# A decoder layer on one core: the first half's experts started inside the last cross-attention batch, with GpSimd splitting the first weights

## What is computed

```python
x = x + self_attention(layernorm(x))           # 16 heads of 64, causal
x = x + cross_attention(layernorm(x), ctx)     # 16 heads of 8, softmax over 256 keys
x = x + ffn(layernorm(x))

# ffn: 8 experts, the best two of each token
scores = xn @ Wr + br;  indicator = one_hot(top_k(scores, 2)).sum(-2)
weights = softmax(where(indicator > 0, scores, -inf))
for i in range(8):
    h   = relu((xn * indicator[..., i:i+1]) @ W1[i] + b1[i])     # 128 -> 512
    out = out + (h @ W2[i] + b2[i]) * weights[..., i:i+1]        # 512 -> 128
```

## Time and profile before

| | us |
|---|---|
| median of 3 runs | 348.15 |
| lowest, highest | 346.92, 350.82 |
| the profiled execution, its time | 347.81 |
| the span of its records | 346.0 |
| outside the span | 1.81 |

### The profile page before, as it was taken

How to read it: one execution, slowest core, us unless ns; L and a number is a source line. 1 busy time by engine, 2 the same in 40 slices (tenths; PEclk the granted TensorE clock), 3 DMA queues, 4 the chain that set the end, 5 groups by cost and what they waited for, 6 DMA issues and landing times.

```text
span 346.0 us, 5393 instructions
## 1 busy us (share of the span) xinstructions
PE 301.5 (87%) x1852; PEld 212.2 (61%) x1869; DVE 214.7 (62%) x452; ACT 190.4 (55%) x525; POOL 91.2 (26%) x130
## 2 busy tenths in 40 slices
PE   6799999999988997988688367776999999799995
PEld 2677777767865784556234123334778678578884
DVE  4768563746488848745877267446766876556661
ACT  2679767478466634664365258684553454336350
POOL 7990550320112009302400490313421300000000
PEclk9999999999999998999899699999999999899999
DMA  8800035501000100010029920000000000100001
GB/s 244 175 2 2 2 52 67 66 3 45 0 2 13 35 1 3 3 46 2 3 64 366 282 72 4 2 0 2 0 1 2 0 1 0 32 0 0 3 0 30
DMA packets 14911, 14.06 MB, mean 41 GB/s; under 512 B 2643, under 2 KB 10915, under 8 KB 14883
## 3 DMA queue, kind: packets, MB, share of 16 engines
q1 hardware_dynamic: 13300, 12.92, 15.1%
q10 hardware_dynamic: 1584, 0.80, 0.8%
HBM read 9.94 MB, written 0.52 MB: 30 GB/s over the span
## 4 chain that ended last, share of the span: by engine, by line
PE 65%; DVE 16%; DMA 4%; ACT 4%; issue 3%; SPq 3%; POOL 2%; another core or an unknown queue 0%; DVEq 0%; ACTq 0%; POOLq 0%
PE ps L592 6%; PE ps L594 6%; PE ps L593 6%; PE ps L666 6%; PE ps L699 4%; PE ps L711 4%; PE ps L868 4%; PE ps L869 4%; PE ps L870 4%; DMA w_raw<-in_L_ffn_b 3%; PE ps L744 3%; DVE mneg L1233 3%; PE ps L780 3%; PE ps L673 2%; PE ps L701 2%
## 5 line engine op out<-in xcount | busy, mean ns | idle before, releaser
L987 ACT ACTIVATE p<-ps,negmax 128x256 f32<-128x256 f32 (+1 forms) x128 | 52.6, 425 | 26.5 <-DVE negmax L1202 26.2
L1314 DVE SCALAR_TENSOR_TENSOR hid_lo<-ps,hid_hi 128x512 fp32r<-128x512 f32 x64 | 41.8, 685 | 23.3 <-ACT hid_hi L1051 23.3
L1233 DVE TENSOR_REDUCE mneg<-ps 128x2 f32<-128x512 f32 x64 | 42.3, 683 | 21.6 <-PE ps L744 20.9
L1016 ACT ACTIVATE px<-ps 128x512 f32<-128x512 f32 x64 | 35.1, 598 | 23.9 <-PE ps L765 22.1
L1202 DVE TENSOR_REDUCE negmax<-ps 128x2 f32<-128x512 f32 (+1 forms) x48 | 33.0, 687 | 20.6 <-PE ps L668 13.2
L1051 ACT ACTIVATE hid_hi<-ps 128x512 fp32r<-128x512 f32 x64 | 35.0, 596 | 8.1 <-PE ps L594 7.6
L744 PE MATMUL ps<-k_st,q_mem 128*128 128x256 bf16 x128 | 25.5, 283 | 12.3 <-DVE mneg L1233 11.5
L1046 ACT CAST x_hi<-x_f 128x512 fp32r<-128x512 f32 x16 | 9.9, 620 | 38.8 <-DVE x_f L1304 38.8
L973 ACT CAST t_hi<-ps 128x512 fp32r<-128x512 f32 x32 | 18.7, 591 | 19.5 <-PE ps L594 18.5
L592 PE MATMUL ps<-x_hi,w_hi 128*128 128x512 f32 x64 | 26.4, 412 | 2.2 <-DVE hid_lo L1314 1.4
L987 ACT ACTIVATION_READ_ACCUMULATOR p<-ps,negmax 128x1 f32 x128 | 26.6, 208 | 0.0
(11 more groups left out here) (191 smaller groups left out, 665.1 us busy)
## 6 DMA issues: line engine op xcount, KB each, us to landing
w_raw<-in_L_ffn_W SPq DMA_DIRECT2D x1, 2048.0 KB, 8.6
w_last<-in_L_ffn_W SPq DMA_DIRECT2D x1, 2048.0 KB, 14.5
k_st<-k_part SPq DMA_DIRECT2D x12, 128.0 KB
q_mem<-q_part SPq DMA_DIRECT2D x48, 32.0 KB
w_in<-in_L_attn_W_qkv ACTq DMA_DIRECT2D x2, 384.0 KB, 6.3
...
```

The source lines that it names most:

```text
L987: last = act.activation(dst, bank[:, n * i:n * i + n], ACT.Exp, bias=negmax[:, kt, h:h + 1], accum_out=psums[:, kt, h:h + 1])
L1016: act.activation(px[:, (g // 2) % 2, c0:c0 + 512], ps[:, k % 3, :], ACT.Exp, scale=SCALE_X).then_inc(s_px, 1)
L1233: dve.tensor_reduce(mneg[:, qt, :].rearrange("p (r g) -> p r g", r=2)[:, :, g], ps[:, max_bank[("MX", b, u)], :].rearrange("p (h k) -> p h ...
L1314: dve.scalar_tensor_tensor(hid[1][:, k % 2, c, :], ps[:, H_BANK[c], :], 0.0, hid[0][:, k % 2, c, :].bitcast(F32), ALU.max, ALU.subtract).t ...
```

## The change

1. **Memory.** `hid` keeps one run instead of two, both parts in the place of `q_mem0`, so that `q_mem1` (batches 2 and 3) stays whole while experts run. `w1_last` becomes a ring of three experts.
2. **Order.** `WS` moves from the eight slots of batch 2 to slots (1, 4), (1, 6), (2, 6) and expert runs 0 to 4. In batch 2 the output units of batch 1 and in batch 3 those of batch 2 come a slot earlier, `NT(0)` moves to (2, 7), `RT(0)` to (3, 0), `GT(0)` to (3, 2), `WT(0)` to (3, 3), `X(0)` to (3, 4). Slots 6 and 7 of batch 3, their `CO`, and `oT0`, `oT1`, `wo` of batch 2 and all output units of batch 3 stand between the chunks of runs 0 to 2. `W2` and the units of the second half shift likewise.
3. **Second product by chunks.** `Y(k-1, c)` stands ahead of `H(k, c)`, for each c. `relu_high` waits for the one chunk it overwrites.
4. **Banks.** Batch 3's scores use two banks instead of three, runs 0 and 1 have two hidden banks instead of four, and the last two output products share bank 3.
5. **GpSimd.** The low part of W1 is made on GpSimd (`first_low`) instead of DVE; `first_weights`, `first_low`, `second_weights` and `norm_3` alternate in a written order. PE waits for the low part of its own expert only.
6. **SP's queue.** Three last rows instead of all at once, then b2, a wait for W1, b1, the maxima of batch 2, W2, two last rows, the maxima of batch 3, the other three.

```diff
+LAST_RING = 3
...
-        w_in, q_mem0, hid_hi = overlay([("w_in", 4096, F32)], [("q_mem0", 8192, BF16)], [("hid_hi", 4096, F32R)])
+        w_in, q_mem0, hid_hi, hid_lo = overlay([("w_in", 4096, F32)], [("q_mem0", 8192, BF16)],
+                                               [("hid_hi", 2048, F32R), ("hid_lo", 2048, F32R)])
...
-        wk_mem, g_hi, ctxT, k_f, q_mem1, hid_lo = overlay(
+        wk_mem, g_hi, ctxT, k_f, q_mem1 = overlay(
             [("wk_blk", 2048, F32), ("g_hi", 2048, F32R)], [("ctxT", 1024, F32), ("k_f", 1024, F32)],
-            [("q_mem1", 8192, BF16)], [("hid_lo", 4096, F32R)])
-        hid = [w[:, :].rearrange("p (r c n) -> p r c n", r=2, c=NC) for w in (hid_hi, hid_lo)]
+            [("q_mem1", 8192, BF16)])
+        hid = [w[:, :].rearrange("p (c n) -> p c n", c=NC) for w in (hid_hi, hid_lo)]
...
-        px, w1_last, _, w2_hi, g_lo, t_hi, t_lo = overlay(
-            [("px", 4096, F32), ("w1_last", 4096, F32)], [("px_too", 4096, F32), ("w2_hi", 4096, F32R)],
+        px, w2_hi, g_lo, t_hi, t_lo = overlay(
+            [("px", 4096, F32), ("w2_hi", 4096, F32R)],
             [("g_lo", 2048, F32R), ("t_hi", 3072, F32R), ("t_lo", 3072, F32R)])
...
+        w1_last = sb("w1_last", [P, LAST_RING, HID])
...
+            if b == last:
+                units = [("oq0", b - 1), ("oq1", b - 1)]
             tail = {}
-            for g, unit in zip((2, 3, 4, 5, 5) if b else (0, 0, 1, 2, 3, 5, 6), units):
+            for g, unit in zip(((0, 0, 1, 2, 3, 5, 6), (2, 3, 4, 5, 5), (1, 2, 3, 4, 4), (1, 2))[b], units):
                 tail.setdefault(g, []).append(unit)
-            more = {(3, 0): [("NT", 0)], (3, 1): [("RT", 0)], (3, 3): [("GT", 0), ("W2", 0, 0)], (3, 5): [("W2", 0, 1)],
-                    (3, 6): [("WT", 0)], (3, 7): [("X", 0)]}
+            more = {(1, 4): [("WS", 0, 0)], (1, 6): [("WS", 0, 1)], (2, 6): [("WS", 0, 2)], (2, 7): [("NT", 0)],
+                    (3, 0): [("RT", 0)], (3, 2): [("GT", 0)], (3, 3): [("WT", 0), ("W2", 0, 0)], (3, 4): [("X", 0)]}
             for g in range(HP):
...
+                if (b, g) < (last, 6):
+                    slots.append(slot)
+
+        beside = {(0, 0): [("CS", last, 6, 0), ("CS", last, 6, 1), ("CO", last, 2)],
+                  (0, 1): [("CS", last, 7, 0), ("CS", last, 7, 1), ("oT0", last - 1)],
+                  (0, 2): [("oT1", last - 1)], (0, 3): [("CO", last, 3), ("wo", last - 1)],
+                  (1, 0): [("oq0", last)], (1, 1): [("oT0", last)], (1, 2): [("oq1", last)], (1, 3): [("oT1", last)],
+                  (2, 0): [("wo", last)], (4, 0): [("NT", 1)], (4, 2): [("RT", 1)], (5, 1): [("GT", 1)],
+                  (6, 1): [("WT", 1)], (9, 1): [("YO", 0, 0)], (9, 2): [("YO", 0, 1)]}
+        for k in range(2 * NE + 1):
             slot = [("YE", 0, 0), ("YE", 0, 1)] if k == NE + 1 else []
             slot += [("X", k + 1)] if k + 1 < 2 * NE else []
             for c in range(NC):
-                slot += [("H", k, c)] + beside.get((k, c), [])
-            if k + 2 < NE:
-                slot += [("W2", 0, k + 2)]
+                slot += [("Y", k - 1, c)] if k else []
+                slot += [("H", k, c)] if k < 2 * NE else []
+                slot += beside.get((k, c), [])
+                if c == 0 and k + 3 < NE:
+                    slot += [("WS", 0, k + 3)]
+                if c == 2 and k + 1 < NE:
+                    slot += [("W2", 0, k + 1)]
             if k % NE == 2:
                 slot += [("B2", k // NE)]
-            slots.append(slot + ([("Y", k - 1)] if k else []))
-        slots.append([("Y", 2 * NE - 1), ("YE", 1, 0), ("YE", 1, 1), ("YO", 1, 0), ("YO", 1, 1)])
+            slots.append(slot)
+        slots.append([("YE", 1, 0), ("YE", 1, 1), ("YO", 1, 0), ("YO", 1, 1)])
...
-        G_BANK, H_BANK, Y_BANK = (0, 1, 2, 7), (0, 1, 2, 5), (3, 4)
+        G_BANK, Y_BANK = (0, 1, 2, 7), (4, 3)
+
+        def score_bank(b, k):
+
+            return k % 3 if b < B - 1 else k % 2
+
+        def out_bank(m):
+            return 3 + m % 2 if m < 2 * B - 1 else 3
+
+        def hidden_bank(k, c):
+            return (2, 5)[c % 2] if k < 2 else (0, 1, 2, 5)[c]
+
+        def last_in(bank, users):
+            return max((n for n, used in users if used == bank), default=-1)
+        score_banks = [score_bank(k // (2 * HP), k) for k in range(2 * HP * B)]
+        hidden_banks = [hidden_bank(n // NC, n % NC) for n in range(2 * NE * NC)]
...
-            sp.dma_start(w1_last[:, :].rearrange("p (e n) -> p e n", n=HID), w1[:, LAST, :].partition_broadcast(P)
-                         ).then_inc(s_wlast, 16)
+
+            def last_rows(i):
+                if i >= LAST_RING:
+                    sp.wait_ge(s_wdiff, i - LAST_RING + 1)
+                sp.dma_start(w1_last[:, i % LAST_RING, :], w1[i, LAST, :].partition_broadcast(P)
+                             ).then_inc(s_wlast[i % LAST_RING], 16)
+
+            for i in range(LAST_RING):
+                last_rows(i)
             sp.wait_ge(s_zero, 1)
             for r in (0, LOW):
                 sp.dma_start(b2_sb[r:r + NE, :], b2).then_inc(s_b2, 16)
+            sp.wait_ge(s_w12[0], 16)
+            sp.dma_start(w1_raw[LAST:D, :], b1.rearrange("e n -> (e n)").unsqueeze(0)).then_inc(s_b1, 16)
             stack_m(2)
             sp.dma_start(w2_raw[:, :].rearrange("p (n d) -> p n d", d=D), w2.rearrange("e (c p) d -> p (e c) d", p=P)).then_inc(s_w12[1], 16)
-            sp.wait_ge(s_w12[0], 16)
-            sp.dma_start(w1_raw[LAST:D, :], b1.rearrange("e n -> (e n)").unsqueeze(0)).then_inc(s_b1, 16)
+            last_rows(3)
+            last_rows(4)
             stack_m(3)
+            for i in range(5, NE):
+                last_rows(i)
             for hf in range(2):
                 for i in range(2):
                     ts = slice(4 * hf + 2 * i, 4 * hf + 2 * i + 2)
...
                     pool.wait_ge(s_w12[0], 16)
-                    pool.wait_ge(s_wlast, 16)
+                pool.wait_ge(s_wlast[i % LAST_RING], 16 * (i // LAST_RING + 1))
                 cols = slice(512 * i, 512 * i + 512)
-                pool.tensor_tensor(w1_raw[0:LAST, cols], w1_raw[0:LAST, cols], w1_last[0:LAST, cols], ALU.subtract
-                                   ).then_inc(s_wdiff, 1)
+                pool.tensor_tensor(w1_raw[0:LAST, cols], w1_raw[0:LAST, cols], w1_last[0:LAST, i % LAST_RING, :],
+                                   ALU.subtract).then_inc(s_wdiff, 1)
+
+            def first_low(i):
+                pool.wait_ge(s_whi, i + 1)
+                cols = slice(512 * i, 512 * i + 512)
+                pool.tensor_tensor(w1_lo[:, cols], w1_raw[:, cols], w1_hi[:, cols].bitcast(F32), ALU.subtract
+                                   ).then_inc(s_wlo, 1)
 
             def second_weights(i):
                 pool.wait_ge(s_w2hi, i + 1)
...
-            for i in range(NE):
-                first_weights(i)
+            first_weights(0)
+            first_weights(1)
             norm_3(0)
+            first_low(0)
+            first_weights(2)
+            first_low(1)
             norm_3(1)
+            first_weights(3)
+            first_low(2)
+            second_weights(0)
             norm_3(2)
-            for i in range(3):
-                second_weights(i)
+            first_low(3)
+            first_weights(4)
+            second_weights(1)
             norm_3(3)
-            for i in range(3, NE):
-                second_weights(i)
+            for i in range(4, NE):
+                first_low(i)
+                if i + 1 < NE:
+                    first_weights(i + 1)
+                second_weights(i - 2)
+            second_weights(NE - 2)
+            second_weights(NE - 1)
...
-                e = k % NE
-                if k == 0 and c == 0:
-                    pe.wait_ge(s_wlo, 8)
-                    pe.wait_ge(s_px, 16 * B)
+                e, n = k % NE, NC * k + c
+                bank = hidden_banks[n]
+                if c == 0:
+                    if k < NE:
+                        pe.wait_ge(s_wlo, e + 1)
+                    pe.wait_ge(s_xlo, k + 1)
+                before = last_in(bank, enumerate(hidden_banks[:n]))
+                if before >= 0:
+                    pe.wait_ge(s_hd, before + 1)
+                elif bank < 3:
+                    pe.wait_ge(s_px, last_in(bank, enumerate(score_banks)) + 1)
+                else:
                     pe.wait_ge(s_mx_ev, 16 * B)
+                products(ps[:, bank, :], [w[:, e, P * c:P * c + P] for w in w1_p], [x[:, k % 2, :] for x in x_p]
+                         ).then_inc(s_h, 1)
+
+            def combine(k, c):
+
+                e, hf = k % NE, k // NE
+                bank = ps[:, Y_BANK[hf], :]
                 if c == 0:
-                    pe.wait_ge(s_xlo, k + 1)
-                if k >= 1:
-                    pe.wait_ge(s_hd, 4 * (k - 1) + c + 1)
-                products(ps[:, H_BANK[c], :], [w[:, e, P * c:P * c + P] for w in w1_p],
```

(45 more changed lines are left out.)

33 lines of the change are left out of this document (12 added, 21 removed).

## The result

| | before | after |
|---|---|---|
| median | 347.53 (346.70 to 350.82, 4 runs) | 355.26 (354.09 to 355.65, 4 runs) |
| ratio to before | | 1.0199, interval 1.0127 to 1.0271 |
| the profiled execution, its time | 347.81 | 354.09 |
| its span; mean granted clock | 346.0; 0.975 | 352.3; 0.966 |

The account below looks back on a forecast made before the run. Cross attention was taken as short of ACT time and bound by waits, the experts from about 244 us by PE. Terms 1.8 - 6.1 - 1.7 + 11.1 - 3.0 = +2.1 gave 349.9 us, range 342.5 to 356.

Parts of the forecast that it names:

- Step A: End of batch 1: ACT waits for b1, the stop for the maxima is swapped, not removed; +1.8 us.
- rival 3: Slower: b1's issue takes 7.8 us by itself, batch 2 starts 6 us later than forecast; 356 us, chance 0.10.
- Step B: Batch 2 to the router: stops and weight passes go until the norm comes to rule; -6.1 us.
- the sign of being wrong, 17 us: Batch 2: the prediction is wrong if this batch takes more than 17 us.
- Rival 2: Same time: batch 2 gives all of its 9.0 us; 347.0 us, chance 0.16.
- Step C: Router to first chunk: a chain of 13.7 instead of 15.4 us, first chunk at 230.0; -1.7 us.
- Step D: First chunk to the end of run 3's slot: moved-in PE work and waits, 37.3 against 26.2 us; +11.1 us.
- the clock fall: Among the experts: PE drops to a lower clock after the 4.8 us stop; +1.7 us.
- rival 1: Faster: DVE takes both residuals at once, the stop falls to 2.6 us or less; 344.7 us, chance 0.22.
- Step E: Later experts: clock fall +1.7, gates' wait -1.4, output transposes -1.6 and their fall -1.7; -3.0 us in all.
- The transposes: The two output transposes, two chunks apart instead of one: stop -1.6 us and its clock fall -1.7 us.
- Rival 4: Slower: GpSimd and DVE hinder each other through eight more GpSimd passes, 4 us; 354 us, chance 0.08.

Follow-up runs that it names:

- a4b: The changed kernel with the maxima of batch 2 issued ahead of the wait for W1 and of b1: 354.60 us.
- a5b: The changed kernel with the first two weight passes (WS) in batch 2, slots (2, 0) and (2, 2): 351.01 us.
- a6b: The changed kernel with batch 2's maxima ahead of b1 and the first two WS in batch 2: 347.84 us.
- b2: The kernel before with only SP's queue reordered (three last rows, b2 load, maxima, b1, other rows, W2): 340.37 us.
- c1b: The changed kernel, GpSimd's weights and low parts ahead of norms, batch 2's oq1 a slot later, maxima before b1, two WS in batch 2: 336.68 us.
- d1: The changed kernel with W1's low part on DVE again, GpSimd's order otherwise kept: 351.70 us.
- a1: The changed kernel with first_weights(4) and (5) ahead of norm_3(2) on GpSimd: 353.92 us.
- a3: The changed kernel with oq1 of batch 2 one slot later, in slot 3 of batch 3: 352.11 us.
- b1: The kernel before with only the second product by chunks, Y(k-1, c) ahead of H(k, c): 348.41 us, ratio 1.0008.

## Why the prediction was right or wrong

**Step A, +1.8: right in mechanism, +1.0 measured.** ACT waited for b1 for 5.76 us (to 190.04), PE for 7.03 us ahead of `wo` of batch 1, and batch 2 began 1.0 us later than before; W1 had been issued 0.7 us earlier than before (178.98 and 179.66), so the wait itself cost 1.7. b1's issue took 0.23 us where I had taken 0.7:

```profile
187.39 0.23 SPq L451 DMA_DIRECT2D w_raw<-in_L_ffn_b  x1
187.66 4.09 SPq L425 DMA_DIRECT2D q_mem<-m_part  x6
```

With that, rival 3 is out. That the stop is swapped and not removed was the point of this step, and a4b, a5b and a6b show it.

**Step B, -6.1: right, -6.4 measured.** Batch 2 to the router took 18.0 us against 24.4; its own eight slots took 16.5 (to the first scores of batch 3 at 213.68), so the sign of being wrong, 17 us, did not come. The norm did come to rule, as put: a stop of 1.17 us at 213.22, ended by GpSimd's `norm`. Rival 2's 9.0 us was out of reach for that reason. It belongs to the new places of `WS`: in b2, where all eight stay in batch 2, the stretch took 23.0 us, in a6b and c1b 17.9. The queue and these places gain at different ends, and the changed kernel gave the queue's part away: its router starts at 215.21, that of the kernel before with its queue in order at 215.13.

**Step C, -1.7: wrong, +1.4 measured.** Router to first chunk took 16.8 us, not 13.7, and the first chunk came at 232.0, not near 230. What the step put at nothing is the low clock in cross attention: PE's stops of 1.76 and 2.66 us were each followed by some 3 us at 0.50, and I had priced a clock fall for stops among the experts only. What the falls cost on the path can be read where the same units of PE ran without them:

```profile
226.42 0.75 PE L869 MATMUL ps<-ident,wgt_p 128*40 128x128 f32 x4 [2.66 <-DVE wgt_p L1345]
```

```profile
226.10 0.60 PE L880 MATMUL ps<-ident,wgt_p 128*40 128x128 f32 x4 [2.24 <-DVE wgt_p L1349]
230.77 0.47 PE L648 MATMUL ps<-x_hi,w_hi 128*128 128x512 f32 x1 [0.92 <-issue]
```

The first row is d1's, where the clock stayed full behind the first stop (1.00 in 220.86 to 225.00): the turned gates started 9.3 us after the router (217.10), after the change 10.6. The other two are a4b's, where it stayed full behind the second stop (1.00 in 226.10 to 230.10): from the turned gates to the first chunk took 4.7 us, after the change 6.2; a1 gives 4.7 too. That makes 2.8 of the 3.1 us. The rest of the chain, 9.3 + 4.7 = 14.0 us, was forecast within 0.3, `oq1` and its normalising ahead of the gates included. With `oq1` moved behind the gates (a3, c1b) the stop of 2.66 us and its fall went, and the stretch took 13.6 and 13.7 us. The chain without those 2.2 us would say 11.5; the one fall left there (clock 0.63 in 212.6 to 216.0 of c1b) makes 1.3 of the difference and a stop of 0.74 us right behind the moved `oq1` most of the rest.

**Step D, +11.1, and the clock fall, +1.7: right, the largest term, within 0.1 us by luck.** First chunk to slot 4 took 37.85 us against 25.76, +12.1. The turn `NT(1)` (0.6 us), which I had counted in it, now lies behind the mark; with it +12.7, against 12.8. The stops were forecast at 1.3 + 3.4 + 4.8 = 9.5 and came as 0.57 + 3.13 + 4.62 = 8.3; the fall took 4 us at 0.50, 2.0. So the stops were 1.2 us too long in the forecast, and three things too small made up for them: the fall by 0.3, PE's work and short waits by 0.3, and the baseline, where I had put the end of run 3's slot at 262.2 and it lay at 261.8. The waits of ACT for GpSimd (3.84 and 7.70 us) stand where they were put. PE's stop for `Y(2, 0)` read 4.62 or 4.63 us also in a3, a4b, a5b and a6b, which leave GpSimd's order alone: it is a chain of fixed lengths, and rival 1, that DVE would not be late, never came near.

**Step E without the fall, -4.7: -2.4 measured, with the turn counted in D.** Slot 4 to `X(10)` took 0.7 us longer than before, of which 0.6 is the turn: the gates' -1.4 did not come at all. 1.01 and 0.26 us stand at `WT(1)` and `X(8)` instead of 1.40, so PE was not without stops from run 4 on, as I had put for a sign. The step assumed that chunks of `Y` between the `H` cover a wait for DVE, which b1 refutes. The transposes gave 2.7 of 3.3 us. "Costs nothing later" for W1's low part on GpSimd held from run 3 on but not before, where its pass stood in the chain (d1).

**Rival 4** gave the time within 1.3 us (354), nearer than the forecast of 349.9, by a mechanism that hardly acted: one of sixteen passes was hit, as before, for 1.1 us. That the time alone would speak for it is what d1 was run for.

Together: C 3.1, the gates 1.5, the transposes 0.6 and the tail 0.2 too hopeful, A 0.8, B 0.3 and D 0.1 too dark: 4.2 between +2.1 and +6.3. So the range held the time, but the sum was two thirds short of the loss.
